# Two PSUM banks of another use take the third and fourth V tile of every batch

## The reference

```
q, k, v = x @ Wq.T, x @ Wk.T, x @ Wv.T        # 256, 256 and 512 features, 8 heads
o_preact = x @ Wog.T
i_pre, f_pre = soft_cap(x @ Wig.T + big), soft_cap(x @ Wfg.T + bfg)
h = mlstm_scan(q, k, v, i_pre, f_pre)         # gated, normalised state over the 512 tokens
y = (sigmoid(o_preact) * multihead_norm(h)) @ Wout.T
x = x + y
h = gelu(layernorm(x) @ absmean_quant(w1).T + b1)
x = x + h @ absmean_quant(w2).T + b2
```

## Time and profile before

| | |
|---|---|
| median of 3 runs | 1995.58 us (1993.9 to 1996.75) |
| the profiled execution | 1993.98 us |
| its span | 1992.2 us |
| PE busy | 1848.6 us, 93% |
| VectorE busy | 1277.1 us, 64% |
| ScalarE busy | 1034.1 us, 52% |
| GpSimd busy | 605.3 us, 30% |
| mean granted TensorE clock | 0.978 |

### The profile page before, as it was taken

How to read it: one execution, slowest core, us unless ns; L and a number is a source line. 1 busy time by engine, 2 the same in 40 slices (tenths; PEclk the granted TensorE clock), 3 DMA queues, 4 the chain that set the end, 5 groups by cost and what they waited for, 6 DMA issues and landing times.

```text
span 1992.2 us, 27804 instructions
## 1 busy us (share of the span) xinstructions
PE 1848.6 (93%) x10676; PEld 984.7 (49%) x10676; DVE 1277.1 (64%) x2286; ACT 1034.1 (52%) x1711; POOL 605.3 (30%) x401
## 2 busy tenths in 40 slices
PE   4667999999999999999999999999999999999989
PEld 2353454645445464544546454454645445464544
DVE  3787666675766667576666757666675766656542
ACT  4755727355372735537273553727355371745623
POOL 1333242241324224132422413242240324223030
PEclk7878999999999999999999999999999999999989
DMA  7232324141231514123151412315141241413010
GB/s 259 95 110 84 84 49 130 33 126 30 86 84 48 131 32 126 29 86 85 48 130 32 125 31 85 85 48 131 32 125 22 82 97 49 110 31 105 1 48 22
DMA packets 233508, 156.72 MB, mean 79 GB/s; under 512 B 195088, under 2 KB 199312, under 8 KB 228256
## 3 DMA queue, kind: packets, MB, share of 16 engines
q1 hardware_dynamic: 231792, 151.79, 29.1%
q10 hardware_dynamic: 1584, 3.15, 0.4%
HBM read 90.48 MB, written 17.24 MB: 54 GB/s over the span
## 4 chain that ended last, share of the span: by engine, by line
PE 76%; ACT 12%; DVE 7%; issue 3%; DMA 1%; POOL 0%; SPq 0%; POOLq 0%; DVEq 0%; ACTq 0%
PE pf L1690 22%; PE pf L1676 19%; PE pa L1567 18%; PE pa L1558 8%; PE ph L1649 4%; ACT dec L842 3%; PE ph L1643 2%; PE ph L1605 1%; ACT g L862 1%; ACT L862 1%; ACT L774 1%; ACT L772 1%; ACT vaug L794 1%; DVE dec L1241 1%; DVE mean L1093 1%
## 5 line engine op out<-in xcount | busy, mean ns | idle before, releaser
L1690 PE MATMUL pf<-w2T,gT 128*128 128x512 f16 x2048 | 535.2, 379 | 0.0
L1676 PE MATMUL pf<-x2T,w1T 128*128 128x512 f16 x2048 | 457.7, 381 | 32.7 <-ACT g L862 32.1
L1327 DVE SCALAR_TENSOR_TENSOR gT<-g,wscale,gT 128x512 f16<-128x512 f32 x256 | 192.4, 751 | 266.2 <-ACT gT L865 266.2
L1567 PE MATMUL pa<-wT,xT 128*128 128x512 f16 x1536 | 343.4, 382 | 10.0 <-ACT vaug L794 10.0
L1676 PEld LDWEIGHTS pf<-x2T,w1T 128*128 128x128 f16 x2048 | 198.4, 98 | 270.1 <-ACT g L862 35.2
L1690 PEld LDWEIGHTS pf<-w2T,gT 128*128 128x128 f16 x2048 | 224.3, 111 | 173.9
L580 POOL TENSOR_TENSOR hinv<-hvar,half 128x8 f32<-128x8 f32 x64 | 105.1, 1642 | 668.9 <-DVE hvar L1278 668.9
L566 POOL TENSOR_TENSOR dec<-dec,causal 128x1024 f32<-128x1024 f32 x64 | 172.5, 2725 | 244.3 <-DMA dec<-gate_r 244.2
L1567 PEld LDWEIGHTS pa<-wT,xT 128*128 128x128 f16 x1536 | 148.4, 98 | 196.3 <-ACT vaug L794 17.9
L862 ACT ACTIVATE g<-pf,b1c 128x512 f32<-128x512 f32 x256 | 175.7, 686 | 121.8 <-PE pf L1676 121.6
L870 ACT ACTIVATE ktok<-kT 128x512 f32<-128x512 f32 x64 | 40.3, 630 | 324.0 <-DVE kT L1265 324.0
(11 more groups left out here) (200 smaller groups left out, 2274.4 us busy)
## 6 DMA issues: line engine op xcount, KB each, us to landing
dec<-gate_r SPq DMA_DIRECT2D x32, 1024.0 KB, 5.6
xin<-L_attn_x SPq DMA_DIRECT2D x16, 1024.0 KB, 6.2
out<-x1b SPq DMA_DIRECT2D x64, 256.0 KB, 2.3
xres<-L_attn_x SPq DMA_DIRECT2D x16, 512.0 KB, 6.1
xres<-L_attn_x SPq DMA_DIRECT2D x32, 256.0 KB, 3.3
qw<-gate_w SPq DMA_DIRECT2D x128, 48.0 KB, 5.7
gT<-L_ffn_w SPq DMA_DIRECT2D x5, 1024.0 KB, 4.8
gT<-L_ffn_w ACTq DMA_DIRECT2D x3, 1024.0 KB, 6.4
```

The costliest lines, as they stand in the source:

```text
L1327: nc.vector.scalar_tensor_tensor(gT[:, LO, f, :], g32[:, f % 2, :], wscale[:, W_GELU:W_GELU + 1], gT[:, HI, f, :], ALU.mult, ALU.subtract) ...
L1567: last = nc.tensor.matmul(bank, src[:, xs, k, :], wT[:, ws, k, col:col + D], start=(k == 0 and n == 0), stop=(k == KD - 1 and n == 2))
L1676: last = nc.tensor.matmul(bank, w1T[:, k, tok(f)], x2T[:, part, :, k, :], start=(k == 0 and part == HI), stop=(k == KD - 1 and part == LO))
L1690: last = nc.tensor.matmul(bank, gT[:, part, f, tok(t)], w2T[:, f, :], start=(f == 0 and part == HI), stop=(f == NF - 1 and part == LO), sk ...
```

## The change

The third and the fourth V tile no longer go through `pa`. They are the first two uses of `ph` in a batch: the third tile goes to bank 0 of `ph`, the fourth to bank 1. The use numbers of `pa` from K on fall by two, so that each keeps its bank; those of `ph` rise by two. In the new function `late_values` both tiles take `ph` by `take_ph`, with uses 0 and 1. ACT's `value` reads them there and counts up `ph_free`.

```diff
-    U_GATE, U_V, U_K, U_Q, U_O, U_KLAST = 0, 1, 5, 7, 9, 13
+    U_GATE, U_V, U_K, U_Q, U_O, U_KLAST = 0, 1, 3, 5, 7, 11
...
-    U_GT, U_U, U_H = 0, 1, T
-    PH_USES = 2 * T
+    U_V2, U_GT, U_U = 0, 2, 3
+    U_H = U_U + T - 1
+    PH_USES = U_H + T
...
             def value(b, t):
                 use = U_V + t
-                act.wait_ge(pa_fill, pa_filled(b, use))
-                nc.scalar.activation(vaug[:, t, :, 0:DHV], pa[:, use % 2, :].rearrange("p (h v) -> p h v", v=DHV),
-                                     ACT.Copy, scale=evac[:, W_V:W_V + 1]).then_inc(pa_free[use % 2], 1)
+                if t < 2:
+                    act.wait_ge(pa_fill, pa_filled(b, use))
+                else:
+                    act.wait_ge(ph_fill, at(b, PH_USES, U_V2 + t - 1))
+                bank = pa[:, use % 2, :] if t < 2 else ph[:, t - 2, :]
+                nc.scalar.activation(vaug[:, t, :, 0:DHV], bank.rearrange("p (h v) -> p h v", v=DHV),
+                                     ACT.Copy, scale=evac[:, W_V:W_V + 1]).then_inc(pa_free[use % 2] if t < 2 else ph_free, 1)
...
             def tokens(b, use, src, col):
 
-                bank = take_pa(b, use)
+                token_products(take_pa(b, use), src, col).then_inc(pa_fill, 1)
+
+            def late_values(b, t):
+
+                take_ph(b, U_V2 + t - 2)
+                token_products(ph[:, t - 2, :], xT[:, :, t, :, :], C_V).then_inc(ph_fill, 1)
+
+            def token_products(bank, src, col):
+
                 for k in range(KD):
                     for n, (xs, ws) in enumerate(PARTS):
                         last = nc.tensor.matmul(bank, src[:, xs, k, :], wT[:, ws, k, col:col + D],
                                                 start=(k == 0 and n == 0), stop=(k == KD - 1 and n == 2))
-                last.then_inc(pa_fill, 1)
+                return last
...
                 if j == 0:
                     pe.wait_ge(ps_free[0], at(b, PS_USES[0], 1))
-                    for t in (T - 2, T - 1):
+                    for t in (0, 1):
                         pe.wait_ge(pa_free[(U_V + t) % 2], pa_done(b, U_V + t))
+                    pe.wait_ge(ph_free, at(b, PH_USES, U_V2 + 2))
...
                 for t in range(T):
-                    tokens(b, U_V + t, xT[:, :, t, :, :], C_V)
+                    if t < 2:
+                        tokens(b, U_V + t, xT[:, :, t, :, :], C_V)
+                    else:
+                        late_values(b, t)
```

## The result

The changed kernel takes 2008.02 us (median of 5 runs, 2007.74 to 2013.59) against 1995.58 us before. The ratio is 1.0072, with a 95% interval of 1.0055 to 1.0089; it is the ratio of the means, the medians differ by 12.4 us or 0.62%. The profiled execution took 2009.1 us, its span is 2007.4 us, 15.2 us longer than before. I had forecast +8.7 us.

What follows compares the result with a forecast made beforehand. PE was taken to bound the kernel (76% of the chain of waits). 14 x 0.57 = 8.0 us, batch 1 +0.7 and batch 0 0 gave 8.7 us on the 1995.58 us median: 2004.3 us, range 2001.3 to 2008.8.

Steps and rivals of the forecast that it cites:

- the clock's term: Stretches at 1.2 GHz in the batches: one less to two more, 1.7 us each, so -1.7 to +3.4 us.
- The third tile: 0: Third V tile on PE: its new wait, for the previous batch's last head product, gains and loses nothing, 0 us.
- The fourth tile: +0.57 us: Fourth V tile on PE, batches 2 to 15: waits until ACT has copied the third tile, +0.57 us per batch.
- Batch 1: +0.7: Fourth V tile in batch 1: its start moves from 186.30 to 187.02, +0.7 us.
- Batch 0: 0: Batch 0: fourth V tile starts 1.1 us later, but later PE work waits for weights; 0, upper bound 1.1 us.
- Nothing here takes up the 0.57 us: Rest of each batch after the fourth V tile: no later PE wait absorbs the delay, so the period grows by 0.57 us.
- The rival in which the time does not change: The existing 2.12 us wait for GELU takes up the fourth tile's delay; result 1995.6 us, chance 6%.
- if PEclk falls in more batches: Sign of a wrong prediction in the new profile: PE's granted clock drops in more batches than before.
- The third rival: 1 us idle before the fourth V tile brings 1.2 GHz stretches in half of 15 batches; 2017 us, chance 5%.
- The "faster" rival: The wait at the fourth V tile vanishes because both tiles have unneeded banks; gain 6.2 us, 1989.4 us, chance 2%.

Runs made afterwards that it cites:

- the wait alone: Kernel before, all V tiles still in pa, with one added line making the fourth V tile also wait until the third is copied: 2012.88 us, ratio 1.0089.
- the one with the shortest period: Changed kernel with the fourth V tile waiting only for the previous batch's ph uses, and the first K product copied earlier: 1990.80 us, ratio 0.9986.

## Why the prediction was right in its mechanism and wrong in its size

The median of 2008.02 us lies just inside my range of 2001.3 to 2008.8, the profiled execution of 2009.1 just outside it, and the ratio of 1.0072 above the 1.0066 that the upper end stands for. That the median is still inside is no merit of the clock's term, which is 5 us beyond its own bound: batch 0 and the last stage came out 1.3 us shorter, and the bounds of the other terms left room.

- "The third tile: 0." Right: no wait in its row. The reason given was not: the last head product of the batch before is not "longer ago than the Q, O and scores work of a batch". VectorE's last read of it ends at 981.2 us, 24 us before the tile starts at 1005.05, and that work takes some 32 us. But 24 us are enough.
- "The fourth tile: +0.57 us." Right: 0.56 in batch 8 (8.97 - 8.41), and it needs no new banks, as the wait alone shows. I missed that in two batches the wait is only 0.78 us.
- "Batch 1: +0.7." Right: 10.66 us from the gate product to the fourth tile, 9.95 before.
- "Batch 0: 0." Not contradicted, but one trace of each can't tell, since batch 0 differed by 4 us between two executions of one kernel: batch 1 starts at 176.01 against 176.35. The fourth tile starts 1.2 us later there (54.59 against 53.42), and the work behind it at 58.85, where it waits for the weights, as before. The tile took 4.42 us before, partly at 1.2 GHz, and 2.76 here behind a wait of 3.55 us: even that idle time does not bring a low stretch each time.
- "Nothing here takes up the 0.57 us." Right: ACT's idle time before the fourth O tile is 1.27 us as before. The rival in which the time does not change is refuted by that row.
- The failed step is the term of the clock, "one less to two more such stretches, -1.7 to +3.4 us". It measured +8.45 us, five more stretches. I had read one stretch in 14 batches as an accident with a rate, and taken the rate as lasting. The runs show in its place that the number depends on the length of the batch: three more matmuls per batch, with the same idle times, also give six. The even spacing of the low stretches speaks against chance as well. My own sign of being wrong, "if PEclk falls in more batches", is what happened.
- The third rival ("slower still", 5%) was nearest in the count: it expected low stretches in half of the 15 batches, and six came. Its time of 2017 us is 9 us too high, and its cause is wrong. It put the stretches down to the idle time before the V tile, where the experiment with busy matmuls in that place gives the same six.
- The "faster" rival (2%) had put its gain at 6.2 us. The kernel in which the fourth tile has its own wait is the one that it described, and it gained 2.7, since another wait took the place of the first.

What stays open is why the number of low stretches goes with the period in this way. The runs show that it does, and that the low stretches go when the wait of 2.1 us is shortened to 1.17 us or less. An even spacing would fit the batches drifting against something in the chip that repeats by itself, but no run here tests that. One execution was profiled for each setting, so the counts are uncertain: with one more matmul the profiled execution (1996.78 us, two low stretches) is the fastest of six, 3.5 us under their median.

## What to carry to other kernels

A counter shared by two banks makes the second user wait for the first, so a bank "of its own" needs a wait of its own; and where a wait is removed, the copy behind it may take most of the gain (0.5 of 0.65 us here). In this kernel, which repeats a batch with a PE wait of 2.1 us in it, a change of the batch's length by 0.5% cost nearly as much again through the clock when it made the batch longer, and lost more than half of its gain when it made it shorter. Where a profile shows such a wait, filling it with matmuls, useless ones even, shows what the change itself is worth; in the three kernels tried here the filling also made the kernel faster, by 2.4, 6.1 and 8.2 us.

## What the runs showed of the hardware that was not expected

- More work can be faster: eight matmuls more per batch, 1.73 us in a wait of 2.12, took 2.4 us off the kernel before and 8.2 us off the one with the shortest period.
- A wait of 2.12 us brought stretches at 1.2 GHz in 1 to 6 of 15 batches, each costing 1.69 us in the 32 matmuls behind it (8.77 against 7.08). A wait of 1.17 us brought none in 15.
- How often they came followed the period of the batches, with PE's idle times unchanged: one stretch at 116.20 us, two at 116.42, six at 116.86. The Trainium skill (TensorE: Matmul & The Clock Gate, section "A second HAM failure mode: psum-queue depth-cycling") puts such swings down to small idle times between groups of matmuls. These runs agree in that taking the idle time away ended them, and add that the idle time alone did not tell how often they come.
